# The gram matrix of the channel attention: its lower left block turned from the upper right one

## The reference, cut to what matters

```python
h = group_norm(x, gn_scale, gn_bias)
qkv = jnp.einsum('bchw,oc->bohw', h, qkv_w) + qkv_b[None, :, None, None]
q, k, v = ...                                       # 8 heads of 32 channels each
attn = jnp.einsum('bhcn,bhdn->bhcd', q, k) * dh ** (-0.5)
attn = jax.nn.softmax(attn, axis=-1)
out = jnp.einsum('bhcd,bhdn->bhcn', attn, v)
out = jnp.einsum('bchw,oc->bohw', out, proj_w) + proj_b[None, :, None, None]
return x + out
```

## Time and profile before

| what | value |
|---|---|
| median of three runs | 2928.32 us |
| the profiled execution's own time | 2925.99 us |
| its span | 2924.2 us |
| outside the span | 1.8 us |
| PE busy | 2778.9 us (95%) |
| POOL busy | 2154.3 us (74%) |
| DVE busy | 1863.7 us (64%) |
| ACT busy | 1553.3 us (53%) |
| mean granted TensorE clock | 0.987 |

### The profile page before, as it was taken

The page is one execution under the profiler, slowest core; times in us unless marked ns, Lnnn a source line. Parts: engine busy times, 40 slices in busy tenths (PEclk is TensorE's granted clock), DMA queues, the critical chain, the costliest instruction groups (busy, mean ns, idle before and its releaser), DMA issues.

```text
span 2924.2 us, 35836 instructions
## 1 busy us (share of the span) xinstructions
PE 2778.9 (95%) x12912; PEld 1379.1 (47%) x12912; DVE 1863.7 (64%) x3341; ACT 1553.3 (53%) x2794; POOL 2154.3 (74%) x740
## 2 busy tenths in 40 slices
PE   6879999999999999999999999999999999999998
PEld 4444445544455444554445445454445544444442
DVE  1347776576756667566675676756776566767672
ACT  2225655556555556455564555644655446566554
POOL 3208777688867788687886888858887688887877
PEclk9979999999999999999999999999999999999999
DMA  2060344303434145232450334413343313433340
GB/s 81 25 95 18 47 75 60 51 20 47 88 46 56 24 51 93 33 52 46 53 94 13 46 60 57 76 23 35 60 74 60 48 24 46 75 46 46 46 60 16
DMA packets 74387, 150.85 MB, mean 52 GB/s; under 512 B 9121, under 2 KB 10657, under 8 KB 74210
## 3 DMA queue, kind: packets, MB, share of 16 engines
q1 hardware_dynamic: 74210, 148.56, 33.2%
HBM read 20.46 MB, written 16.78 MB: 13 GB/s over the span
## 4 chain that ended last, share of the span: by engine, by line
PE 70%; ACT 9%; POOL 8%; DMA 6%; DVE 4%; issue 3%; SPq 0%; ACTq 0%; POOLq 0%; DVEq 0%
PE psum L1335 16%; PE psum L1360 12%; PE psum L1304 11%; PE psum L1243 6%; POOL vT L841 5%; PE psum L1274 5%; ACT prob L945 5%; PE psum L1251 4%; PE psum L1356 4%; DMA K<-hi 3%; DMA Q<-max_rows 2%; PE psum L1383 2%; PE psum L1178 2%; POOL acc L841 2%; PE psum L1378 1%
## 5 line engine op out<-in xcount | busy, mean ns | idle before, releaser
L1082 DVE TENSOR_REDUCE maxpart<-psum 128x1 f32<-128x512 f32 x2176 | 1407.1, 684 | 730.2 <-PE psum L1304 705.9
L945 ACT ACTIVATE prob<-psum 128x512 f32<-128x512 f32 x2176 | 1224.8, 596 | 921.9 <-PE psum L1335 886.7
L841 POOL TENSOR_TENSOR acc<-acc,prob 128x2048 f32<-128x2048 f32 (+1 forms) x317 | 1130.3, 3566 | 163.4 <-ACT prob L945 133.9
L1335 PE MATMUL psum<-Q,K 104*128 104x512 f32 x2048 | 1080.7, 529 | 69.4 <-ACT prob L945 41.5
L1304 PE MATMUL psum<-K,Q 96*128 96x512 f32 x2048 | 820.8, 404 | 15.1 <-DVE maxpart L1082 11.6
L1335 PEld LDWEIGHTS psum<-Q,K 104*128 104x128 f32 x2048 | 384.4, 188 | 765.7 <-ACT prob L945 473.9
L841 POOL TENSOR_TENSOR vT<-vT,prob 128x2048 f32<-128x2048 f32 x122 | 556.2, 4559 | 22.5 <-ACT prob L945 12.0
L1360 PE MATMUL psum<-prob,vT 128*32 128x512 f32 x4096 | 555.6, 604 | 0.0
L1304 PEld LDWEIGHTS psum<-K,Q 96*128 96x128 f32 x2048 | 391.9, 191 | 149.3 <-issue 72.4
L841 POOL TENSOR_TENSOR acc<-prob 128x2048 f32<-128x2048 f32 (+1 forms) x58 | 212.3, 3661 | 314.7 <-ACT prob L945 161.9
L1360 PEld LDWEIGHTS psum<-prob,vT 128*32 128x32 f32 x4096 | 97.2, 108 | 197.0 <-ACT prob L945 110.3
(11 more groups left out here) (138 smaller groups left out, 2070.5 us busy)
## 6 DMA issues: line engine op xcount, KB each, us to landing
Q<-hi SPq DMA_DIRECT2D x128, 256.0 KB
K<-hi SPq DMA_DIRECT2D x128, 256.0 KB
Q<-lo SPq DMA_DIRECT2D x64, 256.0 KB
K<-lo SPq DMA_DIRECT2D x64, 256.0 KB
scratch<-xa SPq DMA_DIRECT2D x8, 1024.0 KB, 4.0
xb<-scratch SPq DMA_DIRECT2D x8, 1024.0 KB, 4.8
xa<-in_x SPq DMA_DIRECT2D x7, 1024.0 KB, 8.6
out<-hb SPq DMA_DIRECT2D x7, 1024.0 KB, 5.8
```

The source lines that it names most:

```text
L841: pool.tensor_tensor(total, first if a == 1 else total, this, ALU.add).then_inc(added, 1)
L945: act.activation(prob[STEP_STARTS.slot(b, start)][:, j, :], score_bank[(SCORES.rank[b.n][e] - 1) % SCORE_BANKS], ACT.Exp, scale=1.0 if lay ...
L1082: dve.tensor_reduce(maxpart[layer][:, a // NQ, a % NQ:a % NQ + 1], bank, AX_X, ALU.max).then_inc(max_free, 1)
L1335: pe.matmul(score_bank[(r - 1) % SCORE_BANKS], left, right, start=True, stop=True).then_inc(score_full, 1)
```

## The change

The gram's second half computes only its right 128 columns, the first half all 256, so the upper right block is there and the lower left is not. A new side piece, `cross`, transposes `gram[:, 0, 128:256]` with one TensorE transpose into the next PSUM bank, and ACT copies that to `gram[:, 1, 0:128]`. ACT's copy of the gram's bank becomes two copies (128x256 and 128x128). `cross` needs the gram's copy, `keys` needs that of `cross`. In `spread` the six images' layer 0 has one chunk more (n = 18), and the second image's group (1, 0) has four chunks in place of three.

```diff
-    return ([("side", layer, "gram"), ("side", layer, "keys"), [("side", layer, "logits"), ("softmax0", layer)]]
+    return ([("side", layer, "gram"), ("side", layer, "cross"), ("side", layer, "keys"), [("side", layer, "logits"), ("softmax0", layer)]]
...
-    gram_to_logits, from_attv = rest0[:3], rest0[3:]
+    gram_to_logits, from_attv = rest0[:4], rest0[4:]
...
-             (1, 0, spread(0, 7, rest5[1:3]), [(1, 1, 0, 8, 0, 3), rows(1, 1, 6)]),
-             (1, 1, spread(0, 6, rest5[3:6]), []),
-             gap(cut(rest5[6:7] + out1[:T * NQ + 7] + out5[:2] + out1[T * NQ + 7:T * NQ + 9] + out5[2:]
+             (1, 0, spread(0, 7, rest5[1:4]), [(1, 1, 0, 8, 0, 3), rows(1, 1, 6)]),
+             (1, 1, spread(0, 6, rest5[4:7]), []),
+             gap(cut(rest5[7:8] + out1[:T * NQ + 7] + out5[:2] + out1[T * NQ + 7:T * NQ + 9] + out5[2:]
...
-            for what, need in (("gram", ("turn", KC // 2 - 1)), ("keys", ("gram",)), ("logits", ("keys",)),
+            for what, need in (("gram", ("turn", KC // 2 - 1)), ("cross", ("gram",)), ("keys", ("cross",)), ("logits", ("keys",)),
...
+                            elif what == "gram":
+                                act.copy(gram[layer][:, 0, :], side_bank[:, 0:C])
+                                act.copy(gram[layer][:, 1, P:C], side_bank[:, C + P:2 * C]).then_inc(side_free, 1)
+                            elif what == "cross":
+                                act.copy(gram[layer][:, 1, 0:P], side_bank[:, 0:P]).then_inc(side_free, 1)
...
                         elif what == "gram":
                             for t, kt in share((t, kt) for t in range(T) for kt in range(KC)):
-                                ins = pe.matmul(side_bank[:, t * C:(t + 1) * C], hT[:, kt, t * P:(t + 1) * P],
-                                                hT[:, kt, :], start=(kt == 0), stop=(kt == KC - 1))
+                                ins = pe.matmul(side_bank[:, t * C + t * P:(t + 1) * C], hT[:, kt, t * P:(t + 1) * P],
+                                                hT[:, kt, t * P:C], start=(kt == 0), stop=(kt == KC - 1))
+                        elif what == "cross":
+                            ins = pe.transpose(side_bank[:, 0:P], gram[layer][:, 0, P:C], ident)
```

More of the change, by code:

```diff
@@ L183, in group_sequence @@
     norm5, begin5, rest5 = normalise(NEXT0), channel_attention(True, NEXT0)[-2 - KC // 2:], channel_attention(False, NEXT0)
-    turn5, out5 = begin5[2:], rest5[7:]
+    turn5, out5 = begin5[2:], rest5[8:]
     image0 = channel_attention(True) + rest0
@@ L870, in program @@
                         layer, what = e[1], e[2]
-                        if layer in FIRST and what in ("rows", "turn", "gram", "keys", "attv", "mix"):
+                        if layer in FIRST and what in ("rows", "turn", "gram", "cross", "keys", "attv", "mix"):
                             act.wait_ge(*filled(b, e))
@@ L879, in program @@
                                          side_bank).then_inc(side_free, 1)
+                            elif what == "gram":
[3 more added lines that the diff above has]
+                                act.copy(gram[layer][:, 1, 0:P], side_bank[:, 0:P]).then_inc(side_free, 1)
                             else:
-                                dst = {"gram": gram, "keys": gk, "attv": attv, "mix": mixT}[what][layer]
+                                dst = {"keys": gk, "attv": attv, "mix": mixT}[what][layer]
                                 act.copy(dst[:, :, :].rearrange("p t c -> p (t c)"), side_bank).then_inc(side_free, 1)
```

## The result

The changed kernel took 2911.36 us, the median of six runs (2906.20 to 2914.85); the kernel before, beside it and with the three runs shown ahead, 2927.41 us. The same kernel in eleven more runs came out at 2919.56 us, ratio 0.9973 (0.9961 to 0.9985), 8 us faster. The two intervals don't overlap. What divides them is the subject of the experiments.

A forecast was written before the change was run, and what follows sets the result against it. PE, busy 95% of the span, was taken as the bound. Steady images -7.2, first image -0.8 and second image -0.3 sum to -8.3 us, from a median of 2928.3 to 2920.0 us; range 2916.5 to 2924.5, with rivals 2915.5 to 2927.

The forecast's parts named there:

- the steady images: Six images' gram to keys: narrow records save 1.66 us each, copies, transpose and second wait cost some back; -7.2 us in all.
- Rival 4: More arrives: second image's gram counts too, or early clock falls get shorter; -11.7 us, 2916.6 us; chance 0.08.
- the second image: Gram's saving hidden by DMAs, 0 or at best 0.6 us; with reordered cross, keys and logits, -0.3 us in sum.
- The records: Gram matmuls on PE: 0.216 us at 256 columns, 0.112 at 128; 16 narrowed records save 1.66 us an image.
- Rival 2: Narrow gram records set by weight loads, 0.168 us each; only -2.1 us in all, 2926.2 us; chance 0.05.
- The transpose: Cross on PE, one transpose added per image, taken as 0.11 us.
- The second wait: PE's new stand before keys in steady images, while cross's copy queues behind an exponential on ACT; 0.29 us.
- First wait: PE's stand before cross in steady images, 0.34 us where keys stood 0.29; +0.05 us.
- Waits further on: Behind keys, ACT and POOL were taken to keep no backlog that would swallow the gain, so it counts in full.
- Rival 1: Only part arrives: longer waits at cross and keys, or a later wait; -4.7 us, 2923.6 us; chance 0.22.
- The first image: Nothing else runs: 1.66 us saved from gram to keys, second copy and serial cross step added; net -0.8 us.
- Rival 3: Slower: PE's clock falls behind each of the six steady grams; +9.0 us in sum, 2937.3 us; chance 0.05.

The follow-up runs named there:

- wide: Changed kernel with the gram's second half back at its full 256 columns, all else kept; ratio 1.0000 to the kernel before.
- halves: Changed kernel with the gram's wide and narrow halves as separate pieces, one PSUM bank each, second image's gram in other memory; 2912.28 us, ratio 0.9949 to the kernel before.
- same_slot: Changed kernel with cross moved into the gram's last slot, right behind its last chunk; median 2911.97 us.

## Why the prediction was wrong

Faster was forecast and faster it is; the size and the range failed, for the most part by what the forecast said of runs, and to a lesser part by its sum for a steady image.

**The range left out the clock.** The step that failed is the sentence that took the spread of the three runs before as all that the range had to hold, on top of a forecast that started from their median; the range's low end was 4.5 us under that forecast. One and the same changed kernel had means 6.9 us apart in two sets, with the time lost to the clock 7.2 us apart. The miss of 8.6 us (2911.4 for 2920.0) comes apart so: 3.5 us, because the starting median of 2928.3 lies above the mean of 2924.8 of the 39 later runs of the same kernel; 3.9 us, because the first six runs lost 32.0 us to the clock and those 39 lost 37.0; 1.4 us, because at equal clock the six are 9.7 ± 0.9 us faster and not 8.3; less 0.2 between mean and median. Whether the clock or chance put the early runs of the kernel before so high isn't known, since their clocks aren't listed.

Against the 39 runs before, all 17 of the changed kernel give a difference of means of 9.2 us, and 8.9 ± 0.6 at equal clock. So 8.3 was near for the change itself, and the 16 between medians was the change plus what the clock and the choice of runs added. It was near in part by luck: the steady images gave 1.4 us more than their term, and of the 1.1 us of the two others the total leaves 0.3 ± 0.6. That the lower clock comes more rarely because of the change isn't shown: its 17 runs lost 36.7 us, those before 37.0. What made the falls rarer in the first six stays open. Rival 4 had the direction, with a chance of 0.08, but neither of its forms is what the runs show: the second image gave a few tenths, and up to the third gram the granted clock is 0.94 and 0.93 in the two traces of the kernel before and 0.94 in both of the changed one.

**The records.** The 0.216 and 0.112 us are right: chunks of 0.86 and 0.45 us, and `wide` puts 1.67 us an image back where 1.66 was forecast. Rival 2, bound by weight loads, is refuted by the narrow chunks, which would have taken 0.67. The transpose holds PE for 0.13 us: the maximum starts 0.37 us behind cross, where a score alone takes 0.24. Forecast were 0.11. But its result is out 0.30 us after its start, when PE has stood before it. The prediction had the price on PE about right, and for the steady images no time until the result. The Trainium skill ("TensorE: Matmul & The Clock Gate", Part 4: PE-mode transpose) has about 275 ns inside a kernel, in a passage on bf16. The 0.30 us until this transpose's result are near that; the 0.13 us that it costs PE are not.

**The second wait, mis-sized.** I forecast 0.05 + 0.11 + 0.29 = 0.45 us of cost in a steady image, and it is 1.66 - 1.43 = 0.23. Measured from start to start the three terms are -0.04, 0.13 and 0.14. First wait: cross starts 0.65 us after its maximum, keys before started 0.69 after it, since the two copies overlap. Second wait: it is there, as forecast, but half as long, and for another reason. The forecast had cross's copy stand behind an exponential until 0.87 us after cross. The exponential began 0.26 us ahead of cross (1543.52) and was over at 1544.14, when the result of cross had just come. What keys waits for is the serial way of cross itself: 0.30 us until its result, 0.03, the copy of 0.27, 0.14, in sum 0.74, against 0.60 of PE work (0.37 and 0.23) beside it. The copy of 128 columns is the 0.27 us that I chose. The queue behind the exponential is real in `halves`, where cross runs earlier against it, and there the wait is the 0.28 that I forecast for here. Steady images: -8.6 us for -7.2.

**Waits further on.** Nothing swallowed the gain: from keys to the next gram the last three stretches, with the clock full in both kernels, measure 335.97, 336.16 and 336.39 us before, and 336.02, 336.10 and 336.23 after. Rival 1, a longer wait at keys or further on, is refuted by that and by the wait of 0.14 us at keys.

**The first image.** -0.96 us at full clock (`same_slot`) for -0.8 forecast. In the changed kernel's own traces it is +0.7 and +0.9 us (8.60 and 8.78). The gram's 32 records take 7.14 us in the first of them for 5.49 in `same_slot`, and its first eight have a mean duration of 634 ns where the kernel before's have 384 in the same stretch (25.7 to 29 us): they ran at the lower level. The granted clock of the windows reads 1.00 from 20 to 34 us in both, so the profile's clock, and with it the lost time of the fit, leaves this out.

From 34 to 60 us the granted clock was 0.61 in both traces of the changed kernel and 0.74 in both of the kernel before; from the first gram to the first score of layer 1 they took 67.53 and 67.86 us, and 64.90 and 64.81. `same_slot`, with cross too, had 0.74 and 63.48 us. Two traces each can't tell whether the change makes the early fall longer. Where the start is worth watching is plain: the third gram begins anywhere from 472.6 to 482.7 us in the ten traces.

**The second image.** As forecast, its gram saves next to nothing. The row maxima's first matmul comes 1.6 us earlier against the gram's start, and the second stands for the DMA, now 1.40 us of PE's idle time where it was 0.18 (timeline):

```profile
82.70 0.48 PE L1311 MATMUL psum<-qk 96*128 96x512 f32 x1
...
84.58 0.96 PE L1311 MATMUL psum<-qk 96*128 96x512 f32 x3 [1.40 <-DMA qk<-K]
85.12 4.28 DVE L1087 TENSOR_REDUCE maxpart<-psum 128x1 f32<-128x512 f32 x7 [1.21 <-PE psum L1311]
```

From the gram's start to the first score 16.17 us before, 15.73 and 15.97 in the two traces after, 16.20 in `wide`: 0.2 to 0.4 us of 1.66, inside the 0.6 that I allowed. The reordering behind it can't be read apart from the clock, which differs there between the traces.

**Rival 3.** In the changed kernel's first trace the clock held 1.00 for 25 us behind each of the six steady grams; in the second it held 1.00 behind five and was 0.96 behind the last, where one short fall lies. One such fall lies behind the second steady gram of the kernel before, too. No set of runs lost more than the kernel before by a step of the rival's size.

## What to carry to other kernels

Where one engine is the bound for a whole stretch, the saving is the records' distances times their number, and what is added costs little if the plan has work to put between each step and its copy: 0.47 us of other work was worth 0.47 us. Split the producer so that the first part is being copied while the second is computed (`halves`), and even the wait that was there before goes, though part of it comes back at the next step. Read a wait on PE from start to start, against the same pair where nothing waits: an idle time that the profile doesn't list can still be there, under a modelled end. For a gain of some 0.3%, look at the granted clock of each run before believing a median: two sets of six and eleven runs of one kernel differed by as much as the change was worth.

## What the hardware showed that was not expected

- Runs of one program on one core scatter along the time lost to TensorE's lower clock: 26 to 47 us lost in a span of some 2920 over all 105 runs, slope 0.80 ± 0.04, with 1.9 us of scatter left.
- A matmul behind a transpose can start on time while the transpose's result is still 0.30 us away: cross cost PE 0.13 us, and its reader 0.74.
- ACT begins an instruction about 0.1 us before the one ahead ends: copies of 0.37 and 0.27 us take 0.54 together (1543.09 to 1543.63). The Trainium skill states an overlap of about 93 ns for ACTIVATEs back to back ("ScalarE: Activation LUTs", What ACT_TABLE_LOAD costs); the trace agrees, and shows it for copies too.
- A copy of 128 columns from PSUM takes 0.27 us, of 256 columns 0.37, of 512 columns 0.59.
